# Router logits with the weights stationary and the tokens moving, and the order of the small steps around them

## The reference

```python
x = x + tanh(g_xattn[0]) * L0_xattn(layernorm(x), ctx_1024, ...)   # phase A: 16 heads of 16, ctx in two parts
x = x + tanh(g_ffn[0])   * L0_ffn(layernorm(x), ...)               # phase B: mixture of experts
x = x + tanh(g_xattn[1]) * L1_xattn(layernorm(x), ctx_1024, ...)   # phase C: 16 heads of 128
x = x + tanh(g_ffn[1])   * L1_ffn(layernorm(x), ...)               # phase D: weights looked up in a table of 16

# L0_ffn, the step that the change touches:
router_probs = softmax(flat @ gate_w.T)                 # 16 experts
routing_weights, selected = top_k(router_probs, 4)      # then divided by their sum
comb = sum(one_hot(selected) * routing_weights[..., None], axis=1)
for e in range(16):
    mixed += comb[:, e:e+1] * ((silu(flat @ Wg[e]) * (flat @ Wu[e])) @ Wd[e])
shared = ((silu(flat @ sWg) * (flat @ sWu)) @ sWd) * sigmoid(flat @ shared_gate_w)
return mixed + shared
```

## Time and profile before

| | us |
|---|---|
| median of 3 runs (lowest, highest) | 404.07 (403.46, 405.74) |
| the profiled execution | 404.01 |
| its span, first to last instruction | 402.2 |
| PE busy | 374.7 (93%) |
| PEld busy | 351.7 (87%) |
| DVE busy | 312.0 (78%) |
| ACT, POOL busy | 194.0, 168.9 |

### The profile page before, as it was taken

The page is one execution under the profiler, slowest core; times in us unless marked ns, Lnnn a source line. Parts: engine busy times, 40 slices in busy tenths (PEclk is TensorE's granted clock), DMA queues, the critical chain, the costliest instruction groups (busy, mean ns, idle before and its releaser), DMA issues.

```text
span 402.2 us, 8995 instructions
## 1 busy us (share of the span) xinstructions
PE 374.7 (93%) x3586; PEld 351.7 (87%) x3594; DVE 312.0 (78%) x710; ACT 194.0 (48%) x401; POOL 168.9 (42%) x207
## 2 busy tenths in 40 slices
PE   0989999998999999999999999999999999999996
PEld 0777879887899999999999898999989999999996
DVE  3888878697786786775588988898899799965553
ACT  3577677742523333243356635554653556233332
POOL 4246646342303313123255545457424853632332
PEclk9999999999999999999999999999999999999999
DMA  7902102120000300300200010020001000000000
GB/s 219 337 13 78 57 30 80 34 102 2 0 2 0 133 2 1 132 0 10 75 0 2 6 63 2 2 67 3 2 0 56 3 0 2 2 10 19 27 28 27
DMA packets 7166, 16.33 MB, mean 41 GB/s; under 512 B 1218, under 2 KB 4803, under 8 KB 6740
## 3 DMA queue, kind: packets, MB, share of 16 engines
q1 hardware_dynamic: 7124, 15.75, 11.5%
HBM read 14.70 MB, written 1.05 MB: 39 GB/s over the span
## 4 chain that ended last, share of the span: by engine, by line
PE 60%; DVE 24%; ACT 8%; issue 4%; POOL 2%; DMA 1%; DVEq 0%
PE ps L312 37%; PE ps L1385 7%; DVE work L1656 4%; PE ps L414 2%; PE ps L378 2%; ACT work L1522 2%; DVE work L1173 2%; DVE work L1169 1%; ACT work L1500 1%; PE ps L1406 1%; DMA stage<-in_wA 1%; POOL workr L1304 1%; PE ps L982 1%; DVE workr L1613 1%; PE ps L425 1%
## 5 line engine op out<-in xcount | busy, mean ns | idle before, releaser
L1725 POOL TENSOR_SCALAR work<-work,lut_step,lut 128x344 f32<-128x344 int32 (+1 forms) x60 | 42.2, 715 | 53.6 <-DVE work L1641 52.0
L312 PE MATMUL ps<-wB_hi,workr 128*128 128x256 f32 x224 | 50.8, 293 | 3.0 <-POOL workr L1304 1.8
L312 PE MATMUL ps<-xT_hi,wB_hi 128*128 128x256 f32 x176 | 51.1, 290 | 0.3 <-DVE x L606 0.3
L312 PE MATMUL ps<-xT_lo,wB_hi 128*128 128x256 f32 x176 | 49.7, 282 | 0.0
L312 PE MATMUL ps<-xT_hi,wB_lo 128*128 128x256 f32 x176 | 49.7, 282 | 0.0
L1304 POOL TENSOR_TENSOR workr<-work,workr 128x256 fp32r<-128x256 f32 (+1 forms) x36 | 22.9, 636 | 62.3 <-ACT workr L1105 62.2
L312 PE MATMUL ps<-wN_hi,shared_r 128*128 128x256 f32 x256 | 47.8, 281 | 0.0
L1656 DVE COPY_PREDICATED work<-work 128x1376 f32<-128x1376 int32 (+5 forms) x36 | 42.1, 1168 | 2.2
L312 PEld LDWEIGHTS ps<-wB_hi,workr 128*128 128x128 f32 x224 | 38.2, 189 | 6.0 <-issue 3.3
L312 PEld LDWEIGHTS ps<-wN_hi,shared_r 128*128 128x128 f32 x256 | 40.2, 188 | 0.4 <-DVE shared_r L1618 0.3
L312 PE MATMUL ps<-xT_hi,wM_hi 128*128 128x256 f32 x128 | 36.6, 286 | 2.3 <-ACT work L1481 2.3
(11 more groups left out here) (220 smaller groups left out, 1072.7 us busy)
## 6 DMA issues: line engine op xcount, KB each, us to landing
stage<-in_wC SPq DMA_DIRECT2D x3, 1280.0 KB, 5.6
stage<-in_wB SPq DMA_DIRECT2D x4, 768.0 KB, 4.3
stage<-in_idx SPq DMA_DIRECT2D x4, 536.0 KB, 3.4
work<-in_wC SPq DMA_DIRECT2D x2, 640.0 KB, 7.7
stage<-in_wA SPq DMA_DIRECT2D x2, 512.0 KB, 5.6
out<-x SPq DMA_DIRECT2D x8, 128.0 KB, 1.8
x<-in_x SPq DMA_DIRECT2D x2, 256.0 KB, 4.6
x<-in_x SPq DMA_DIRECT2D x1, 512.0 KB, 9.7
```

The lines of the kernel that those rows point to most:

```text
L312: last = nc.tensor.matmul(out, l, r, start=start and i == 0, stop=stop and i == 2)
L1725: nc.gpsimd.tensor_scalar(lev[:, j, 0:n], bits[:, 0, 0:n], lut_step[:, j:j + 1], lut[:, 2 * j:2 * j + 1], ALU.mult, ALU.add).then_inc(*C[" ...
```

## The change

The logits are made the other way round. The router's columns now stand at the front of `wS`, with 256 further columns of `wS` behind them, so that 128 columns from there can be the stationary operand: 18 of them are logits, and the other 110 rows of the result are not read. The 256 tokens move. That makes 6 matmuls of 256 columns in place of 12 of 18, and a result [18, 256] with the logits in rows. ACT copies it to SBUF (`act_B_logits`, new), and PE turns it back in two transposes (`pe_B_turn`, new), from where DVE reads it as before.

In group 0 the turn stands behind both shifts, and `dve_A_lower(a - 1)` now stands ahead of DVE's copy of the logits. In groups 1 to 3 it stands behind gate and up of pair 0. The halves of the combined weights are moved ahead of those of join 0 on ACT and DVE in groups 1 to 3. In group 0 `front_stats(5)` is moved from behind gated 2 to behind `dve_A_add(a)`, and `front_norm(5)` into the loop, behind join 0. The load of `wS` is cut in two.

```diff
         def wS(w):
-            n = DC * 2 * F
-            return (w[:, 0:n].rearrange("p (c n) -> p c n", c=DC), w[:, n:n + D],
-                    w[:, n + D:].rearrange("p (c n) -> p c n", c=DC))
+            r, n = DC * NL, DC * NL + DC * 2 * F
+            return (w[:, r:n].rearrange("p (c n) -> p c n", c=DC), w[:, n:n + D],
+                    [w[:, c * NL:c * NL + P] for c in range(DC)])
...
-            act.wait_ge(wS_in, 16)
+            act.wait_ge(wS_in, 32)
...
         def logits_B(g):
-            return ps[:, 2 if g else 4, 0:TILES * NL]
+            return ps[:, 2 if g else 4, TG:TG + TILES * NL]
+
+        def logitsT_B(g):
+            return ps[:, 2 if g else 4, 0:TG]
...
         def pe_B_logits(pe, g):
             x_split(pe, 4 + g)
+            for c in range(DC):
+                last = mm3(logitsT_B(g), wr_hi[c], wr_lo[c], xT_hi[:, c, :], xT_lo[:, c, :], c == 0, c == DC - 1)
+            last.then_inc(*Bp["lgT_done"].up())
+
+        def pe_B_turn(pe, g):
+            pe.wait_ge(*Bp["lgT_ready"].at(g, 1))
             for t in range(TILES):
-                for c in range(DC):
-                    last = mm3(logits_B(g)[:, t * NL:(t + 1) * NL], xT_hi[:, c, t * P:(t + 1) * P],
-                               xT_lo[:, c, t * P:(t + 1) * P], wr_hi[:, c, :], wr_lo[:, c, :], c == 0, c == DC - 1)
+                last = nc.tensor.transpose(logits_B(g)[:, t * NL:(t + 1) * NL], lgT[:, t * P:(t + 1) * P],
+                                           ident[0:NL, 0:NL])
             last.then_inc(*Bp["logits_done"].up())
@@ pe_AB
             pe_A_shift(pe, a, 0)
             pe_A_shift(pe, a, 1)
+            pe_B_turn(pe, g)
@@ pe_B
             pe_B_gate_up(pe, g, 0)
+            pe_B_turn(pe, g)
             pe_B_gate_up(pe, g, 1)
@@
+        def act_B_logits(act, g):
+            act.wait_ge(*Bp["lgT_done"].at(g, 1))
+            nc.scalar.copy(lgT, logitsT_B(g)[0:NL]).then_inc(*Bp["lgT_ready"].up())
@@ act_AB
             act_B_tanh(act, g, 0)
+            act_B_logits(act, g)
             act_A_exp(act, a, 0)
@@ act_B
+            act_B_logits(act, g)
             act_B_tanh(act, g, 0)
...
+            act_B_comb(act, g)
             act_B_join(act, g, 0)
-            act_B_comb(act, g)
@@ dve_AB
+            dve_A_lower(dve, a - 1)
             dve_B_logits(dve, g)
-            dve_A_lower(dve, a - 1)
...
             dve_B_gated(dve, g, 2)
-            front_stats(dve, 5, 1)
             dve_A_lower(dve, a)
...
             dve_A_add(dve, a)
-            front_norm(dve, 5, 1)
+            front_stats(dve, 5, 1)
             for k in range(5, EC):
...
                 dve_B_join(dve, g, k - 5)
+                if k == 5:
+                    front_norm(dve, 5, 1)
@@ dve_B
             dve_B_gated(dve, g, 2)
+            dve_B_comb(dve, g)
             dve_B_join(dve, g, 0)
-            dve_B_comb(dve, g)
@@ sync
-            sp.dma_start(wS_in_raw, a["wS"]).then_inc(wS_in, 16)
+            for to, v in ((slice(DC * NL, NWS), slice(0, NWS - DC * NL)), (slice(0, DC * NL), slice(NWS - DC * NL, NWS))):
+                sp.dma_start(wS_in_raw[:, to], a["wS"][:, v]).then_inc(wS_in, 16)
```

More of the change, by code:

```diff
@@ L218, in build @@
         CH = EC + 1
-        Bp = signals("B", dve=12, logits_done=1, shifted=1, exp_ready=1, gate_ready=1, comb_ready=2,
+        Bp = signals("B", dve=12, logits_done=1, lgT_done=1, lgT_ready=1, shifted=1, exp_ready=1, gate_ready=1, comb_ready=2,
                      combT_done=1, combT_hi=1, combT_lo=1, gu_done=CH, tanh_ready=CH, h1=CH, h2=CH, bc_done=CH,
@@ L904, in build @@
         wsum, wrec, whalf, sgate = (take(TILES) for _ in range(4))
+        lgT = take(TG)[0:NL]
         th, h1, h2, h3 = ([take(TG) for _ in range(3)] for _ in range(4))
```

## The result

The changed kernel takes 409.49 us (median of 4 executions, 408.03 to 410.24), the kernel before on the same chip 403.77: 1.0122 times as long, 95% interval 1.0093 to 1.0151. Measured once more with the experiments (c0_after), it was 409.03 for 404.62, ratio 1.0113 [1.0090, 1.0136]. The forecast was 406.1, with a range of 404.5 to 408.0: the sign was right, the size short by 3.4 us.

The account below looks back on a forecast made before the run. PE, busy 93% of the span, was taken to bound the kernel, waiting on DVE in phase B. 404.01 + 2.0 (down 0) + 0.17 (norm) - 0.15 (groups 1 to 3) = 406.0, stated as 406.1 us; range 404.5 to 408.0.

Parts of the forecast that it names:

- What bounds in group 0: Group 0: the chain runs over DVE to phase A's addition, then from 96.65 on it is PE's.
- Group 0 up to spread 0: Group 0: shifts start 0.54 us sooner and the statistics leave DVE's chain, so spread 0 begins 1.52 us sooner, at 91.61.
- Down 0: Group 0: POOL's root awaits late statistics and holds pair 0's lower half; down 0 at 97.87 for 95.33, net +2.0 us.
- the norm: Group 0: the norm moved ahead of weighted 3 on DVE makes PE 0.17 us late at down 5.
- rival (1): Group 0: PE's idle time ahead of down 0 also lowers its clock, costing about 1.3 us; total 407.4, chance 0.23.
- Groups 1 to 3: Groups 1 to 3: one PE wait is traded for another, about 0.05 us saved per group, -0.15 in all.
- The exchange: Groups 1 to 3: combined weights ahead of join 0 start spreads sooner, but join 1 then waits for join 0's half.
- the turn: Two PE transposes with a load each, turning the logits back: 0.22 us of PE, logits copied 0.17 late on DVE.
- Logit matmuls: Each group: six matmuls (0.71) plus turn (0.22) replace twelve (1.34), saving PE 0.41 us, off the chain in groups 1 to 3.
- The load of `wS`: Early load: a second piece half a microsecond behind has 5.7 us of cover before use, so it costs nothing.
- The forecast's own range: Whole kernel: 405.3 to 406.9 us if the forecast case holds, from its terms' ends and 0.3 for POOL's modelled times.

Follow-up runs that it names:

- e1: The changed kernel with statistics and norm of front 5 put back where they stood before in group 0; 405.10 us, ratio 0.9995 to the kernel before.
- e2: The changed kernel with POOL's root of front 5 in group 0 moved behind the lower halves of pairs 0 and 1; 403.76 us, ratio 0.9970.
- e4: The kernel before with only the statistics of front 5 moved behind phase A's addition and the norm behind join 0; 410.14 us, ratio 1.0130.
- e3_warm: The changed kernel with 16 unused matmuls of 512 columns on PE in the idle time ahead of down 0; 407.53 us, ratio 1.0066.
- e11_warm_half: The changed kernel with 8 unused matmuls of 512 columns on PE in the idle time ahead of down 0; 408.35 us, ratio 1.0104.
- e9_logits_alone: The kernel before with only the reversed logits, the turn and ACT's copy, in all four groups; 405.20 us, ratio 1.0013.
- e7: The kernel before with only the combined weights' halves ahead of join 0's in groups 1 to 3, on ACT and DVE; 405.56 us, ratio 1.0014.
- e10: e2 with logits of groups 1 to 3 in the old way and join 1 there behind gate and up 4; 402.18 us, ratio 0.9945.

## Why the prediction was wrong

- **What bounds in group 0, and the place of the loss: right.** The wait on POOL stands where it was put, with the cause that was put down, and e1, e2 and e4 confirm it from three sides.
- **Group 0 up to spread 0, -1.52: right** (91.54 for 91.61). **Down 0, +2.0, and the norm, +0.17: right.** Stall and norm together are 2.08 us (e3_warm), for 2.17; the move without the stall costs 0.22 (e2_root_behind). The norm was never moved by itself.
- **The clock: the step that failed.** The sum held the 4.3 us of idle time but not what it does to the clock; that stood only as rival (1), at 0.23, with "against it speaks that 4.3 is under half of the one seen". That was no reason: nothing in the trace said that less idle time than 9.38 us leaves the clock alone. Its price, 1.3 us, was right (1.30, e3_warm against c0_after); it had to be in the sum, which would then have been 407.4. The price came from the pace of the first matmuls of the span alone, behind the 9.38 us in which there was nothing for PE to do yet the earlier trace rows; the granted clock of the profile reads 1.00 on that very stretch,

```profile
9.40:11.60 2.20, 2.20 (x5) 1.68 (x6) 1.39 (x6) 2.17 (x6) 0.69 (x1) 1.00 1.07 281
```

although the five matmuls take 0.46 each, near the pace of the lower level (0.21 for 256 columns behind the stall). So the slow start stays put down to the clock by its pace only, and that the price came out right is in part luck. The Trainium skill, "TensorE: Matmul & The Clock Gate", section "HAM oscillation — how this bites in real kernels", describes a kernel whose clock drops again with each wait of TensorE for a transfer, of some 3 to 5 us; the idle times of 4.06 and 4.07 us here agree, the 2.21 us of e11_warm_half are shorter than any that it describes. The forecast cited another section of that page and not this one.
- **Groups 1 to 3, -0.05 each: mis-sized, and of the wrong sign.** They got 0.10 longer. The exchange was right (-0.2 by the forecast's own numbers without the late logits, -0.16 measured). The term at fault is the turn. The load of the turned logits comes 0.33 us behind the one before it (116.94 to 117.27), where the stream goes at 0.12, although ACT's copy (L1107, 115.95 to 116.31) was ready almost 1 us before; with its second load it costs PE 0.43 us (117.49 - 116.94 - 0.12), not 0.22. So the logits are copied 0.27 us late (done 2.58 us behind the addition's start, before 112.64 - 110.33 = 2.31), not 0.17, and that is the +0.25 of e9_logits_alone. PE's saving was then 0.17 us a group and not 0.41 (six loads 0.74 and the turn 0.43, for the 1.34 of before): the step "Logit matmuls" failed by the same term, without weight in the sum.
- **The load of `wS`, 0: right** as far as the traces up to tanh 0 tell: c0_after, with one piece more to load, is there at 77.98 for 77.86.
- **The forecast's own range,** 405.3 to 406.9, does not follow from its ends: with -0.41 in each of three groups, 0 for the norm and 0.3 for POOL's times the lower end is near 404.6.
- **Outside all steps:** 1.29 us of the profiled execution up to tanh 0, the fall of the clock at 28 us. It comes and goes (c0_after does not have it; e1, e2, e7 and e10 have one that begins between 59 and 60 us, e4 one at 76 us). The sum was made against one execution that had no such fall, where four of ten have one; the median of the runs is above such a sum for any kernel. And 0.37 us behind the last addition, which does belong to the change: from there to the end of the span it is 3.5 to 3.9 us in all eleven profiles of kernels with the reversed logits in group 0 and the divided load, 3.0 to 3.2 in the three without. SyncE's last two issues take 1.07 us in c0_after for the 0.81 of the kernel before; what makes them longer is open.

Of the 5.6 us the forecast's steps had 2.0; the clock behind the idle time is 1.5 in this execution (3.60 - 2.08), groups 1 to 3 are 0.45 more than forecast (+0.31 for -0.15), 0.37 are the last transfers, and 1.3 belong to the profiled execution. The profile of c0_after, with one fall only, closes without these: 406.0 of the forecast, 1.3 for the clock, 0.4 for groups 1 to 3 and 0.35 for the last transfers make 408.1, and it took 408.22. Seven of the ten executions of the changed kernel took 409.0 us or more, at mean clocks of 0.994 or less; the one of them that was profiled has two falls, and a second one is likely in the others.

## What to carry to other kernels

When work is moved to a later place on one engine, look up who waits for it on the others and what is queued behind that waiting instruction: here one root that nobody needed soon held a product that everyone needed, and moving it behind two others turned a loss of 1.2% into a gain of 0.3%. An idle time of TensorE has two prices, its length and the lower clock behind it, 1.3 us here; put both into the sum where the idle time is as long as the 2.2 and 4.1 us here. A saving on an engine that waits in that stage is worth nothing, and the step that pays for it (a turn, a copy) is paid in full if it lies on the path of the engine that is late.

## What the runs showed of the hardware

- The moment of the fall varies, and it can lie behind the idle time as well as in it. With down 0 as zero the granted clock fell at +0.35 us in the changed kernel, at +1.1 in c0_after and at +0.8 in e11_warm_half, while PE was busy all the time; in e4_move_alone it fell at -0.4, 3.7 us into the idle time:

```profile
100.50:100.80 0.30, 0.00 (x0) 0.00 (x1) 0.00 (x0) 0.00 (x0) 0.30 (x2) 0.50 0.00 0
```

- It also falls with much shorter idle times. In e2_root_behind PE was busy 0.90 and 0.43 of the time in the two microseconds from 58 to 60 us (idle times of 0.40 us up to 57.05 and 0.67 us up to 59.57), the clock fell at about 59.6, and PE then ran at the lower level for over 6 us. The profile of c0_after has 0.38 and 0.74 us of idle time at the same place and no fall:

```profile
58.00:59.00 1.00, 0.90 (x33) 0.76 (x28) 0.33 (x2) 0.66 (x1) 0.78 (x2) 1.00 0.00 0
59.00:60.00 1.00, 0.43 (x7) 0.43 (x7) 0.00 (x0) 0.00 (x0) 1.00 (x3) 0.76 0.00 0
60.00:66.00 6.00, 6.00 (x83) 4.58 (x80) 3.86 (x6) 1.61 (x2) 3.06 (x2) 0.50 0.33 95
```

- Two transposes of an 18-row operand in a running stream cost 0.43 us (group 1 of the changed kernel), half of it a gap ahead of the first load; what makes the gap is open.
